# Subtracting the maximum on VectorE for one unit of attention in four, in a fused cross-attention and mixture-of-experts kernel

## What is computed

```python
q, k, v = proj_split(layernorm(x), W_Q), proj_split(ctx, W_K), proj_split(ctx, W_V)
scores = einsum('bhqd,bhkd->bhqk', q, k) / sqrt(16)
attn = softmax(scores, axis=1)                 # over the 8 heads
x = x + einsum(heads(einsum('bhqk,bhkd->bhqd', attn, v)), W_O)
logits = layernorm(x) @ Wr + br                # top 2 of 8, gates = softmax of the two
h = relu(layernorm(x) @ W1[e] + b1[e])
x = x + sum_e gates[e] * (h @ W2[e]) + gates @ b2
```

## Time and profile before

| | us |
|---|---|
| median of 3 runs (209.5 to 210.3) | 210.16 |
| span of the profiled execution, first to last instruction | 207.8 |
| TensorE busy | 199.5 (96%) |
| VectorE busy | 167.8 (81%) |
| ScalarE busy | 132.2 (64%) |
| GpSimd busy | 112.3 (54%) |

### The profile page before, as it was taken

The page is one execution under the profiler, slowest core; times in us unless marked ns, Lnnn a source line. Parts: engine busy times, 40 slices in busy tenths (PEclk is TensorE's granted clock), DMA queues, the critical chain, the costliest instruction groups (busy, mean ns, idle before and its releaser), DMA issues.

```text
span 207.8 us, 4986 instructions
## 1 busy us (share of the span) xinstructions
PE 199.5 (96%) x1752; PEld 176.5 (85%) x1752; DVE 167.8 (81%) x453; ACT 132.2 (64%) x316; POOL 112.3 (54%) x132
## 2 busy tenths in 40 slices
PE   6999988798999999999999999999999999999995
PEld 6845976686799979997999799998998899789994
DVE  6398769889789999899788988898999888556633
ACT  2236748697568847797677767677757776345441
POOL 8502647869976378629561966376746674010000
PEclk9999999999999999999999999999999999999999
DMA  6649595716515133423140504241000000000000
GB/s 175 160 127 286 153 279 148 224 46 183 158 62 145 69 108 106 103 76 104 41 147 25 170 3 151 57 144 36 0 0 28 0 2 3 25 3 2 25 3 25
DMA packets 20264, 18.70 MB, mean 90 GB/s; under 512 B 1776, under 2 KB 18704, under 8 KB 20240
## 3 DMA queue, kind: packets, MB, share of 16 engines
q1 hardware_dynamic: 17344, 16.85, 28.0%
q10 hardware_dynamic: 2896, 1.54, 2.8%
HBM read 11.83 MB, written 6.55 MB: 88 GB/s over the span
## 4 chain that ended last, share of the span: by engine, by line
PE 91%; DVE 3%; ACT 2%; issue 1%; POOL 1%; POOLq 0%; ACTq 0%; DVEq 0%
PE y_ps L436 28%; PE h_ps L421 22%; PE score_ps L361 7%; PE misc_ps L380 6%; PE score_ps L349 6%; PE h_ps L369 4%; PE score_ps L277 3%; PE misc_ps L401 2%; PE score_ps L338 2%; PE score_ps L421 2%; PE misc_ps L389 2%; PE misc_ps L287 1%; PE misc_ps L327 1%; PE misc_ps L306 1%; PE misc_ps L300 1%
## 5 line engine op out<-in xcount | busy, mean ns | idle before, releaser
L695 ACT ACTIVATE hT<-h_ps,b_sb 128x256 f32<-128x256 f32 x118 | 49.4, 470 | 33.3 <-PE h_ps L421 32.1
L436 PE MATMUL y_ps<-w_sb,hT 128*128 128x128 f32 x508 | 68.0, 277 | 0.0
L436 PEld LDWEIGHTS y_ps<-w_sb,hT 128*128 128x128 f32 x508 | 62.8, 191 | 3.5 <-issue 2.2
L1188 POOL TENSOR_TENSOR half_sum<-e_sb 128x512 f32<-128x512 f32 x28 | 37.3, 1332 | 30.8 <-ACT e_sb L667 30.5
L938 DVE TENSOR_TENSOR attn<-e_sb,e_rcp 128x1024 f32<-128x1024 f32 x32 | 42.1, 1319 | 3.3 <-ACT e_rcp L678 3.3
L930 DVE TENSOR_REDUCE shift_m<-score_ps 128x128 fp32r<-128x1024 f32 x32 | 38.7, 1212 | 2.2 <-PE score_ps L338 1.1
L421 PE MATMUL h_ps<-x1T_hi,w_lo 128*128 128x256 f32 x118 | 37.7, 320 | 1.5 <-ACT hT L695 0.9
L667 ACT ACTIVATE e_sb<-score_ps 128x1024 f32<-128x1024 f32 x32 | 32.8, 1024 | 5.6 <-PE score_ps L361 5.4
L1007 DVE SCALAR_TENSOR_TENSOR acc<-y_ps,gates,acc 128x128 f32<-128x128 f32 x96 | 29.0, 342 | 8.6 <-PE y_ps L436 7.3
L421 PE MATMUL h_ps<-x1T_hi,w_hi 128*128 128x256 f32 x118 | 33.1, 280 | 0.0
L421 PE MATMUL h_ps<-x1T_lo,w_hi 128*128 128x256 f32 x118 | 33.1, 280 | 0.0
(11 more groups left out here) (117 smaller groups left out, 291.3 us busy)
## 6 DMA issues: line engine op xcount, KB each, us to landing
k_scratch<-k_parts SPq DMA_DIRECT2D x14, 256.0 KB, 2.6
k_stack<-k_scratch SPq DMA_DIRECT2D x14, 256.0 KB, 4.0
q_stack<-q_scratch SPq DMA_DIRECT2D x28, 128.0 KB, 2.7
q_scratch<-q_parts SPq DMA_DIRECT2D x7, 256.0 KB, 2.7
w_sb<-in_w SPq DMA_DIRECT2D x1, 1024.0 KB, 6.6
out_y<-y_out SPq DMA_DIRECT2D x7, 128.0 KB, 1.9
x_all<-in_x ACTq DMA_DIRECT2D x1, 768.0 KB, 6.2
ctxT<-in_ctx_t SPq DMA_DIRECT2D x1, 640.0 KB, 6.1
```

The lines of the kernel that those rows point to most:

```text
L436: mm = nc.tensor.matmul(product(j, t), hT[:, j % 2, c, t * P:(t + 1) * P], w2_sb[:, e * HC + c, :], start=(c == 0), stop=(c == HC - 1))
L695: op = nc.scalar.activation(hT[:, j % 2, c, :], hidden(j)[:, c * S:(c + 1) * S], ACT.Relu, bias=b1_sb[:, e * HC + c:e * HC + c + 1])
L1188: nc.gpsimd.tensor_tensor(half_sum[:], e[:, 0:HQ // 2], e[:, HQ // 2:HQ], ALU.add).then_inc(sum_step, 1)
```

## The change

For unit 2 of batches 1 to 7 VectorE itself subtracts the maximum, directly behind `head_max`, from PSUM into `e_sb[:, 2]`; ScalarE then takes the exponential in place in SBUF; TensorE's two matmuls for that unit are gone. Every list keeps its order otherwise. The other 25 units are as before.

```diff
+    VECTOR_UNITS = (2,)
+    FIRST_VECTOR = 1
...
+        def vector_shifts(n):
+            return n >= UNITS * FIRST_VECTOR and n % UNITS in VECTOR_UNITS
+
+        def shifts_on_vector(n):
+            return sum(vector_shifts(k) for k in range(n))
...
             def subtract_max(b, u):
+                if vector_shifts(UNITS * b + u):
+                    return
...
             def exponentiate(b, u):
                 n = UNITS * b + u
-                act.wait_ge(shifted, n + 1)
+                if vector_shifts(n):
+                    act.wait_ge(vector_shifted, shifts_on_vector(n + 1))
+                    nc.scalar.activation(e_sb[:, u, :], e_sb[:, u, :], ACT.Exp, scale=SCALE).then_inc(exp_made, 1)
+                    return
+                act.wait_ge(shifted, n + 1 - shifts_on_vector(n))
...
                                         AX.X, ALU.max).then_inc(max_made, 1)
+                n = UNITS * b + u
+                if vector_shifts(n):
+                    dve.wait_ge(max_made, n + 1)
+                    wait(dve, attn_made, n - 3)
+                    nc.vector.tensor_tensor(e_sb[:, u, :].rearrange("p (h q) -> p h q", h=H),
+                                            score_ps[:, u % 2, :].rearrange("p (h q) -> p h q", h=H),
+                                            shift_m[:, u % 2, :].bitcast(F32).unsqueeze(1).to_broadcast([P, H, P]),
+                                            ALU.subtract).then_inc(vector_shifted, 1)
```

More of the change, by code:

```diff
@@ L142, in build @@
         v_done, v_taken = sem("v_done"), sem("v_taken")
-        scores_done, max_made, shifted, exp_made = (
-            sem("scores_done"), sem("max_made"), sem("shifted"), sem("exp_made"))
+        scores_done, max_made, shifted, vector_shifted, exp_made = (
+            sem("scores_done"), sem("max_made"), sem("shifted"), sem("vector_shifted"), sem("exp_made"))
         sum_step, sum_made, pe_sum_made, log_made, rcp_made, attn_made = (
```

## The result

The changed kernel takes 213.87 us (median of 5 executions, 211.19 to 214.03) against 209.57 for the kernel before, in the same set: a ratio of 1.0168, 95% interval 1.0117 to 1.0219. Two later sets gave 1.0126 (1.0084 to 1.0168) and 1.0140 (1.0097 to 1.0184). A ratio leaves out executions over 1.5% above the fastest of their kernel and is not the quotient of the two medians. By the medians the change costs 2.8 to 4.3 us, by the ratios 2.6 to 3.5; I had said 1.3. The median lies above the top of my range (213.2); the two later medians, 212.82 and 213.03, lie in it.

What follows compares the result with a forecast made beforehand. TensorE (96% busy) was taken as the bound, with the order of VectorE's work deciding. +1.1 - 0.25 + 0.78 - 0.6 + 0.25 = +1.28 us on 210.16 gave 211.5 us; 8-in-10 range 209.3 to 213.2.

Steps and rivals of the forecast that it cites:

- Direction and mechanism: Whole kernel: slower, since VectorE's later instructions hold TensorE up by more than the removed matmuls give; forecast case's chance 0.46.
- The relief: TensorE, unit 2 of batches 1 to 7: seven removed matmul pairs at 0.46 us each, 3.2 us if nothing else is late.
- Size of the subtraction: VectorE: each added subtraction takes 1.21 us, bounds 1.2 and 1.76; with its wait everything behind moves by 1.24 us.
- Batch 1, +1.1: `x1T_lo` and TensorE start 0.80 to 0.82 later, `project_k(3)` waits some 0.3 more; ends +0.8 and +1.4 us.
- my cases: TensorE's relief wins (chance 0.13), a wash (0.27), the forecast (0.46), VectorE's queue becomes the bound (0.14).
- Batch 2, -0.25: TensorE loses the pair, and `project_out(1)`, waiting for `add_b2`, starts at about 55.42 instead of 55.69: -0.25 us.
- but for about 0.05: Batch 2: VectorE's 1.19 us wait for TensorE behind an `add_expert` hides the 1.24 us delay except about 0.05.
- Batch 3, +0.78: `project_k(5)` waits 1.24 us for the residual, the pair behind it saves 0.46: +0.78 us.
- Batches 4 to 6, -0.6: `expert_down(g, 2)` waits for the delayed `add_expert(g, 0)`; of 0.46 TensorE keeps 0.2 per period, three times: -0.6 us.
- Batch 7, +0.25: `add_expert` ends at 162.49, so `expert_down` starts at 162.55 instead of 162.34: +0.25 us with the first-load cost.
- Sum: Whole kernel: the batch terms add up to +1.28 us on the median of 210.16, giving 211.5 us.

Runs made afterwards that it cites:

- e3: The changed kernel with the subtraction moved to VectorE for unit 2 of batches 4 to 7 alone: 210.57 us, ratio 1.0034 to the kernel before.
- e7: As e3, but VectorE subtracts behind `add_expert(g, 0)` instead of in front of it: 209.17 us against 209.95 for the kernel before, ratio 0.9960.
- e4: The changed kernel without any subtraction of the maximum for unit 2 of batches 1 to 7: 207.70 us, ratio 0.9894 to the kernel before.
- e6: The changed kernel with the subtraction moved to VectorE for unit 2 of batch 3 alone: 210.61 us, ratio 1.0027 to the kernel before.
- e1: The changed kernel run again, unaltered: 212.82 us, beside the kernel before at 210.05 us.
- e8: The kernel before plus one unused VectorE reduction from SBUF behind unit 2's maximum in batches 4 to 7: 213.46 us, ratio 1.0171.

## Why the prediction was right or wrong

- **Direction and mechanism: right.** VectorE's queue takes more than TensorE's relief gives. e3 against e7 shows it: the same instructions in another place are 0.7% apart. The relief, put at up to 3.2 us, is 2.35 alone (e4). That the two profiled spans differ by 1.5 us, close to my 1.28, is luck: 0.92 us of an early start hide the rest.
- **Size of the subtraction: right.** 1.21 forecast, 1.224 measured. With its wait it moved the next maximum by 1.26 us (37.75 - 35.35 = 2.40 against 1.14 before), forecast 1.24; `x1T_lo` came 0.82 late, forecast 0.80 to 0.82. Of what the prediction sets against the Trainium skill ("VectorE: DVE Perf Modes", "The DRAIN you can't avoid"), only the cost of the wait differs. The same section says that a next op that is not held starts earlier, and the overlap of 0.08 us agrees with that.
- **Batch 1, +1.1: right in the trace** (+1.14), with the lock between `normalize` and `half_sum` in it (2.19 us: `normalize` ended 1.08 us behind `half_sum`). The Trainium skill ("SBUF — State Buffer", "Who interferes with whom") has this lock, between a VectorE instruction with two SBUF inputs and a GpSimd instruction that reads SBUF. The trace agrees, and the new subtraction, with one SBUF input, kept to 1224 to 1225 ns beside GpSimd. Read against executions in which the weights come late, the term is smaller (e3).
- **Batch 1's idle stretch: missed.** None of my cases had the clock in it, though I had worked out that TensorE would stand idle for longer. In 14 of 17 executions of the changed kernel the clock was 0.984 to 0.992, and a traced dip costs 0.80 us. Filling the stretch takes the dips away (12 of 12 executions), but the medians move by 0.1 us or less. So that the idle stretch makes the dips is shown; what they cost in the median is not.
- **Batch 2, -0.25: wrong, -0.02.** The step "but for about 0.05" failed. The two `add_expert` stand end to end, since the second waits for the first one's semaphore; `add_b2` came 0.18 late, so that `project_out(1)` started only 0.13 earlier. Behind the wait it then took 0.71 us instead of 0.61 (55.79 against 55.69), and the rest was gone.
- **Batch 3, +0.78: right** (+0.79; e6 alone +0.79).
- **Batches 4 to 6, -0.6: too much, -0.14.** The term was mis-sized at the release. I took 0.05 to 0.09 us from the end of `add_expert` to TensorE's start; it is 120.67 - 120.52 = 0.15, and the group then takes 0.97 to the next start instead of the 0.89 of before (119.85 to 120.74). Of 0.46 remain 0.05.
- **Batch 7, +0.25: too little, +0.37**, for the same reason.
- **The last stores: missed.** +0.3 us behind the last matmul, with no cause shown.
- **Sum.** 1.14 - 0.02 + 0.79 - 0.14 + 0.37 = 2.14 us in place of 1.28. With 0.3 for the last stores and 0.80 for the dip that is 3.24 us against the one profiled execution of before, which did not wait for its weights. The three sets measured 4.3, 2.77 and 2.95 by the medians, 3.5, 2.65 and 2.9 by the ratios. What the first set has more is not explained by any trace.

## What to carry to other kernels

Work taken off the bounding engine pays only if the engine that takes it has slack before the next thing that the bound one waits for; read that slack at the place (end of the producer to start of its consumer, less the release), not from busy shares: here 1.38 us of it against 1.24 us of work still left only a tenth of the gain, as the gain itself needs slack too. Put such work behind the instruction that the bounding engine needs, not in front. And if a change leaves TensorE idle for longer than before, look at the granted clock of several executions, not of one profile.

## What the runs showed of the hardware

- In the trace of e1 TensorE's clock fell to 0.50 (1.2 GHz) once it had work again, behind 2 us with 0.27 us of work. In 14 of 17 executions of that kernel the mean clock was 0.984 to 0.992; in the first trace it was 1.0, behind a wait of the same length (1.75 us). A wait of 1.20 us at batch 3 was not followed by a fall in twelve executions.
- A reduction over 8 strided columns of fp32, 128x128 from 128x1024, took 2.01 to 2.03 us from SBUF (four, e8) and 1.19 to 1.23 from PSUM (32, kernel before).
- From the end of the VectorE instruction to TensorE's start it took 0.15 us behind `add_expert` and 0.06 behind `x1T_lo` (38.88 + 0.41 = 39.29, then 39.35).
- The load of the weights for `expert_down` took 5.9 to 6.9 us from issue to landing in fourteen traces; in four of them TensorE waited for it, 0.1 to 1.0 us.
- The profiled executions differ by up to 2.6 us before anything changed is reached (`x1n` of batch 0 at 36.17 to 38.79), about as much as the executions of one kernel differ. A single execution says little; aligned traces say much.
